# A two-layer attention kernel on one core: three accumulating transfers and five GpSimd additions a chunk, and a reordered passage between the layers

## The reference

```python
x = x + L0(_gn(x)); x = x + L1(_gn(x))
# _gn: subtract the mean and divide by the deviation over (H, W, 6 channels), for 32 groups
# L0, outlook attention: a = softmax over 9 taps of x @ W_attn (6 heads); v = x @ W_v
#   y[pos, head] = sum over the 9 taps of a[pos, head, tap] * v[pos + tap]; then y @ W_proj
# L1, shifted 7x7 window attention, 12 heads of 16: q, k, v; softmax(q k / 4 + bias + mask) v; then a projection
```

## Time and profile before

| what | value |
|---|---|
| median of three runs | 3894.26 us |
| profiled execution: its own time, its span | 3895.59 us, 3893.4 us |
| granted TensorE clock, mean | 0.941 of full |
| PE, DVE, ACT, POOL busy | 3493.4, 2794.1, 1905.6, 2423.8 us |
| one pass of the loop (first L1305 at 234.4, last at 3557.3 us, 7 passes between) | 474.7 us |
| in the second pass: outlook stage, passage to the first scores | 572.7 to 709.2 us, 709.2 to 743.8 us |

### The profile page before, as it was taken

How to read it: one execution, slowest core, us unless ns; L and a number is a source line. 1 busy time by engine, 2 the same in 40 slices (tenths; PEclk the granted TensorE clock), 3 DMA queues, 4 the chain that set the end, 5 groups by cost and what they waited for, 6 DMA issues and landing times.

```text
span 3893.4 us, 107608 instructions
## 1 busy us (share of the span) xinstructions
PE 3493.4 (90%) x39716; PEld 1962.9 (50%) x39716; DVE 2794.1 (72%) x4865; ACT 1905.6 (49%) x4034; POOL 2423.8 (62%) x1878
## 2 busy tenths in 40 slices
PE   3989989899798997989989899899998989988998
PEld 3346643466444664346633566335663356533665
DVE  2967759677596776957769577686767767687775
ACT  2435644355443654345643465435554355543565
POOL 0667737677375773757737577376764667555774
PEclk8999989899898998989989899899999999998998
DMA  3642217322272223712236122461225512164121
GB/s 77 132 87 64 78 45 139 74 66 80 59 139 62 71 68 74 141 49 77 75 71 135 48 72 76 88 127 49 75 62 100 113 52 78 55 121 93 60 73 58
DMA packets 206334, 317.58 MB, mean 82 GB/s; under 512 B 18904, under 2 KB 178136, under 8 KB 205784
## 3 DMA queue, kind: packets, MB, share of 16 engines
q0 software_dynamic: 31104, 148.65, 19.5%
q1 hardware_dynamic: 168992, 160.51, 13.9%
q10 hardware_dynamic: 5688, 1.11, 0.2%
HBM read 45.97 MB, written 38.54 MB: 22 GB/s over the span
## 4 chain that ended last, share of the span: by engine, by line
PE 59%; issue 11%; DVE 11%; ACT 8%; POOL 6%; DMA 2%; ACTq 0%; DVEq 0%; POOLq 0%
PE P L433 5%; PE P L625 5%; PE P L642 4%; PE P L294 4%; PE P L296 4%; PE P L596 4%; DVE prod L1280 3%; PE P L575 3%; PE P L303 3%; PE P L578 2%; PE P L302 2%; PE P L660 2%; POOL sp__70 L1566 2%; ACT kbd L988 2%; PE P L297 2%
## 5 line engine op out<-in xcount | busy, mean ns | idle before, releaser
L1559 POOL TENSOR_TENSOR sp__70<-sp__70,mx 128x588 f32<-128x588 f32 x512 | 600.7, 1173 | 622.0 <-DVE mx L1351 621.3
L1280 DVE TENSOR_TENSOR prod<-P,vpad 128x896 f32<-128x896 f32 (+1 forms) x784 | 802.0, 1046 | 133.0 <-PE P L433 120.6
L1566 POOL TENSOR_TENSOR sp__70<-sp__70,rc 128x588 f32<-128x588 f32 x512 | 601.6, 1175 | 55.3 <-DVE rc L1361 55.3
L1341 DVE TENSOR_TENSOR sp__70<-P,relb 128x196 f32<-128x196 f32 x512 | 184.5, 360 | 499.5 <-PE P L596 499.3
L1015 ACT ACTIVATE pt<-P 98x294 f32<-98x294 f32 x1024 | 431.3, 422 | 199.8 <-PE P L625 197.1
L1480 POOL DMA_DIRECT2D prod<-prod x216 | 202.7, 958 | 499.1 <-DVE prod L1280 495.7
L433 PE MATMUL P<-at,sel 108*128 108x448 bf16 x1512 | 426.4, 361 | 58.7 <-DVE prod L1280 30.5
L625 PE MATMUL P<-ident,sp__70 113*98 113x113 f32 x3072 | 399.2, 267 | 48.6 <-POOL sp__70 L1566 35.8
L1358 DVE TENSOR_REDUCE sm<-sp__70 128x12 f32<-128x588 f32 x512 | 387.2, 756 | 45.1 <-ACT sp__70 L1005 44.7
L625 PEld LDWEIGHTS P<-ident,sp__70 113*98 113x98 f32 x3072 | 329.7, 131 | 145.0 <-POOL sp__70 L1566 71.4
L1351 DVE TENSOR_REDUCE mx<-sp__70 128x12 f32<-128x588 f32 x512 | 389.5, 761 | 9.4
(11 more groups left out here) (197 smaller groups left out, 7503.1 us busy)
## 6 DMA issues: line engine op xcount, KB each, us to landing
prod<-prod POOLq DMA_DIRECT2D x216, 672.0 KB, 5.4
vbd<-vs SPq DMA_DIRECT2D x512, 147.0 KB
xin<-in_x SPq DMA_DIRECT2D x126, 336.0 KB, 4.1
out<-ot SPq DMA_DIRECT2D x184, 168.0 KB, 2.3
out<-ot SPq DMA_DIRECT2D x80, 84.0 KB
wn<-in_L_conv_qkv_weight SPq DMA_DIRECT2D x2, 432.0 KB, 6.4
wno<-in_L_conv_proj_weight SPq DMA_DIRECT2D x2, 144.0 KB, 6.5
self<-in_sel ACTq DMA_DIRECT2D x3, 91.1 KB
```

The lines of the kernel that those rows point to most:

```text
L1280: tt(by_row(dst), by_row(P[:, b:b + len(op), 0:CT]), val, ALU.mult).then_inc(prod_ok, 1)
L1559: tt(per_head(sp_[:, b, :]), per_head(sp_[:, b, :]), spread(mx[:, b, :]), ALU.subtract).then_inc(t_sub, 1)
L1566: tt(per_head(sp_[:, b, :]), per_head(sp_[:, b, :]), spread(rc[:, b, :]), ALU.mult).then_inc(p_norm, 1)
```

## The change

Two things are changed together. In the outlook stage the fourth transfer goes (MERGES = 3) and slots 6 and 7 are each added by POOL, so that there are five additions a chunk; for the last chunk the products of tap 8 stay in PSUM and DVE adds slots 7 and 6 and `psum_p` to them there, while POOL makes one addition in place of three. In the passage, a mean of the groups is estimated from the first four chunks during the last one (`mu0`), the final moments about it need one round of matmuls, each tile is aggregated as soon as its statistics are there, the normalization of row 0 is shared between DVE and ACT, keys are made before queries, the first exponentials come before the values are kept, and the second half of row 0's values moves into step 4 of row 0.

```diff
-MERGES = 4
+MERGES = 3
+TAIL, EARLY = 7, 4
-FREED = {0: 1, 2: 1, 3: 2, 4: 3, 6: 4}
+FREED = {0: 1, 2: 1, 6: 2, 3: 3, 4: 4, 7: 5}
...
+            def over_group(j, dst, src):
+                for n, (block, k) in enumerate(GROUPS[j]):
+                    last = mm(dst, gm[:, block, :], src(k), start=(n == 0), stop=(n == len(GROUPS[j]) - 1))
...
# PE, outlook(c), last chunk
+                        elif n in (4, 5, 6):
+                            estimate(n - 4)
+                            if n == 11:
+                                pe.wait_ge(e_kept, ONE + i + 1)
                             stay_warm(2, SOFT_BANK)
...
-                stay_warm(6, SOFT_BANK)
-                group_means(2 * i + 1, SOFT_BANK)
-                group_variances(2 * i + 1, SOFT_BANK)
+                stay_warm(10, SOFT_BANK)
+                group_moments()
                 stay_warm(8, 0)
...
# PE, window stage
@@ ring @@
-                        pe.wait_ge(vs_kept, ONE + 4 * (R + 1))
+                        pe.wait_ge(vs_kept, ONE + 4 * R + (4 if w else 2))
                     elif s == 4:
+                        pe.wait_ge(k_kept, ONE + T * (R + 1) + 3)
...
+                        else:
+                            window_values(0, 1, (R0, R1))
@@ start of the window stage @@
+                first_keys((0, 1))
+                keys_middle(0, 2)
                 queries_wide(0, (R0, R1))
                 queries_middle(0, TURN_BANK)
-                keys_wide(0, (0, 1))
-                keys_middle(0, 2)
                 pe.wait_ge(vs_zero, ONE + 3 * i + 3)
                 for s in range(AHEAD):
                     scores(0, s)
                 window_values(0, 0, (R0, R1))
-                window_values(0, 1, (TURN_BANK, Y_BANK))
-                pe.wait_ge(vs_kept, ONE + 4 * NW * i + 4)
# ACT
-                deviation(2 * i + 1, SOFT_BANK)
+                act.wait_ge(g_two, ONE + 3 * (i + 1))
+                go(gstd[:], gsq[:], ACT.Sqrt, bias=eps_s[:]).then_inc(g_std, 1)
...
+                go(xw[:, 0, 0, :]..., xa[:, 0, ...]..., ACT.Identity, bias=gb[:, 0:1], scale=ga[:, 0:1]).then_inc(xw_zero, 1)
                 load_table(4 * i + 3, ACT.Exp)
...
+                keep_keys(0, 0, 0)
+                keep_keys(0, 1, 1)
+                keep_keys(0, 2, 2)
                 keep_queries(0, 0, R0)
                 keep_queries(0, 1, R1)
                 keep_queries(0, 2, TURN_BANK)
...
+                exp_step(0, 0)
+                exp_step(0, 1)
                 act.wait_ge(vs_zero, ONE + 3 * i + 2)
                 for m in range(2):
                     keep_window_values(0, 0, m, (R0, R1)[m])
# DVE, product and finish_last of the last chunk
+                    if k == KK - 1 and c == LAST:
+                        tt(by_row(P[:, b:b + len(op), 0:CT]), by_row(P[:, b:b + len(op), 0:CT]), val, ALU.mult
+                           ).then_inc(prod_ok, 1)
+                        return
...
+                    two, one = P[:, 0:2, 0:CT], P[:, 2, 0:CT]
+                    tt(two, two, seven[:, 0:2, :], ALU.add).then_inc(tail_ok, 1)
+                    tt(one, one, seven[:, 2, :], ALU.add).then_inc(tail_ok, 1)
+                    tt(two, two, six[:, 0:2, :], ALU.add).then_inc(tail_ok, 1)
+                    tt(one, one, six[:, 2, :], ALU.add).then_inc(tail_ok, 1)
+                    dve.wait_ge(padd_ok, ONE + PADD * (G + 1))
+                    for j in (1, 0, 2):
+                        tt(y0[:, j, :], P[:, j, 0:CT], psum_p[:, j, :], ALU.add).then_inc(tail_ok, 1)
# DVE, in the last chunk after operation 2: three bn_aggr over EARLY chunks; after operation 8: mu0 <- PSUM
+                def moments():
+                    g = 2 * i + 1
+                    tt(gd[:, :, 0], mv[:, :, 0], mu0[:], ALU.subtract).then_inc(g_dev, 1)
+                    tt(gdev[:], gd[:, :, 0], gd[:, :, 0], ALU.mult).then_inc(g_dev, 1)
+                    tt(gd[:, :, 1], gdev[:], mv[:, :, 1], ALU.add).then_inc(g_sq, 1)
+                    mean, square = (P[:, SOFT_BANK, e:2 * T:2] for e in range(2))
+                    nc.vector.tensor_copy(gmean[:], mean).then_inc(g_two, 1)
+                    tt(gdev[:], gmean[:], gmean[:], ALU.mult).then_inc(g_two, 1)
+                    tt(gsq[:], square, gdev[:], ALU.subtract).then_inc(g_two, 1)
+                    tt(gmean[:], gmean[:], mu0[:], ALU.add).then_inc(g_dev, 1)
...
-                for j in range(T):
+                for j in (1, 2):
# POOL
+                    if k in (2, 4):
+                        pool.wait_ge(merged[k // 2], 16 * (G + 1))
+                    else:
                         pool.wait_ge(prod_ok, ONE + NOPS * G + LAST_OP[k] + 1)
...
                 def outlook(c):
                     if c > 0:
-                        add(c - 1, 1, 8)
-                        add(c - 1, 2, 4)
+                        add(c - 1, 2, 8)
+                        add(c - 1, 3, 4)
                     merge(c, 0)
+                    if c == LAST:
+                        merge(c, 1)
                     if c > 0:
-                        add(c - 1, 3, 6)
-                    merge(c, 1)
+                        add(c - 1, 4, 7)
+                    if c < LAST:
+                        merge(c, 1)
                     merge(c, 2)
                     add(c, 0, 2)
-                    if c < CHUNKS - 1:
-                        merge(c, 3)
+                    if c < LAST:
+                        add(c, 1, 6)
...
+                pool.wait_ge(merged[2], 16 * (G0 + CHUNKS))
+                tt(psum_p[:], psum_p[:], slot(4), ALU.add).then_inc(padd_ok, PADD - 1)
```

More of the change, by code:

```diff
@@ L117, in mixer @@
         gmean = sb("gmean", [128, T])
+        mu0 = sb("mu0", [128, T])
+        gd = sb("gd", [128, T, 2])
         gsq = sb("gsq", [128, T])
@@ L304, in middle @@
                 return mm(P[HI, bank, 0:n], w[:, 2, col:col + 64], src[:, 2], start=False, stop=True)
[L306 to L311, removed]
+            GROUPS = (((0, 0), (4, 1)), ((1, 1), (3, 0), (6, 2)), ((2, 2), (5, 1)))
+            def over_group(j, dst, src):
+                for n, (block, k) in enumerate(GROUPS[j]):
+                    last = mm(dst, gm[:, block, :], src(k), start=(n == 0), stop=(n == len(GROUPS[j]) - 1))
                 return last
@@ L315, in group_means @@
                 pe.wait_ge(g_agg, ONE + T * (g + 1))
-                over_groups(bank, 0, mv[:, :, 0]).then_inc(g_mean, 1)
+                for j in range(T):
+                    last = over_group(j, P[:, bank, j:j + 1], lambda k: mv[:, k, 0:1])
+                last.then_inc(g_mean, 1)
             def group_variances(g, bank):
                 pe.wait_ge(g_sq, ONE + g + 1)
-                over_groups(bank, T, gsq).then_inc(g_var, 1)
+                for j in range(T):
+                    last = over_group(j, P[:, bank, T + j:T + j + 1], lambda k: gsq[:, k:k + 1])
+                last.then_inc(g_var, 1)
             def stay_warm(n, bank):
@@ L511, in project, with estimate, group_moments @@
                         project_middle(1)
+                def estimate(j):
+                    if j == 0:
+                        pe.wait_ge(e_agg, ONE + T * (i + 1))
+                    last = over_group(j, P[:, SOFT_BANK, j:j + 1], lambda k: mv[:, k, 0:1])
+                    if j == T - 1:
+                        last.then_inc(g_mean, 1)
+                def group_moments():
+                    pe.wait_ge(g_sq, ONE + 2 * i + 2)
+                    for j in range(T):
+                        last = over_group(j, P[:, SOFT_BANK, 2 * j:2 * j + 2], lambda k: gd[:, k, :])
+                    last.then_inc(g_var, 1)
                 def outlook(c):
@@ L1042, in ring @@
                             keep_out(w - 2, 3, R1)
+                    elif s == 4:
+                        if w == 0:
+                            for m in range(2):
+                                keep_window_values(0, 1, m, (R0, R1)[m])
                     elif s == 5:
@@ L1103, in _ @@
                     keep_window_values(0, 0, m, (R0, R1)[m])
-                exp_step(0, 0)
-                for m in range(2):
-                    keep_window_values(0, 1, m, (TURN_BANK, Y_BANK)[m])
-                exp_step(0, 1)
                 for w in range(NW):
@@ L1288, in outlook @@
                             stat_x1(c - 2, n // 5)
+                        if c == LAST and n == 2:
+                            dve.wait_ge(x1_stat, ONE + T * (G0 + EARLY))
+                            nc.vector.memset(fence[:], 0.0)
+                            for j in range(T):
+                                nc.vector.bn_aggr(mv[:, j, :], stats[:, j, 0:EARLY, :].rearrange("p c s -> p (c s)")
+                                                  ).then_inc(e_agg, 1)
+                        elif c == LAST and n == 8:
+                            dve.wait_ge(g_mean, ONE + 2 * i + 2)
+                            nc.vector.tensor_copy(mu0[:], P[:, SOFT_BANK, 0:T]).then_inc(e_kept, 1)
                         if more:
```

(9 more changed lines are left out.)

88 lines of the change are left out of this document (43 added, 45 removed).

## The result

The changed kernel takes 3923.42 us, median of four runs (3921.29 to 3925.81), against 3893.32 us before in the same comparison: a ratio of 1.008, 95% interval 1.0065 to 1.0095. It is 30 us slower. The profiled execution, the fastest of the four, has a span of 3919.4 us, 26.0 us more than before.

What follows compares the result with a forecast made beforehand. POOL waiting on its own transfer was taken to bound the outlook stage: +13.8 us there, -11.0 in the passage, +2.8 a pass, times 8 = +22 on 3895, rounded to 3920 us; range 3850 to 3965.

Steps and rivals of the forecast that it cites:

- The bound: Outlook stage: POOL waits for its own transfer in a ring of 19.6 us, DVE's period; that idle time cannot be filled.
- The signs named ahead: Outlook stage: POOL's first addition every 21.9 us, released by DMA; DVE waits 2.3 us a chunk; last product at 150 us.
- The ring's size: Outlook stage: POOL part 15.9 us plus landing 5.83 to 6.1, taken as 21.9 us; last product +13.8 us a pass.
- What the ring consists of: Outlook stage: POOL's additions and transfer 1 with its landing; transfer 0 counted only as an issue of 0.61 us.
- The price list: Trainium skill's fit for a GpSimd transfer: 3.6 us, ring about 20.1 us, total 3848 us; traced shortest landing 5.2 us.
- (a to c): Passage from D, the last product's end: sums in PSUM -4.5 us, projection at full clock -1.0, single moments round -4.5.
- (d, e): Passage, into row 0: keys first -0.9 us, exponentials ahead of the copies of values -3.9 us.
- (f): Row 0: second half of values in step 4, so PE waits for their copies; +3.8 us, bounds +1 and +6.
- Total of the passage: From last product through row 0, gains less what row 0 gives back: -11.0 us a pass, -8 to -13.5.
- the ring is hidden or short: Rival, outlook stage: ring under 21.3 us, faster; 3848 us at 20.1 us, 3807 us wholly hidden; chance 0.23.
- stalls cool PE in the outlook stage: Rival: PE waits some 2.3 us in each chunk and its clock drops, much slower, 3970 us; chance 0.12.

Runs made afterwards that it cites:

- e5: Changed kernel with transfer 0 issued ahead of the addition of tap 4 and transfer 1 ahead of that of tap 7, same instructions; 3829.38 us.
- e6: Changed kernel with transfer 1 carrying one of its three tiles, the other two left out of the sum; 3832.75 us.
- e3: Kernel before with three transfers and five additions, keeping its own last chunk and passage; 4004.73 us, ratio 1.0286.
- e1: Changed kernel with transfer 1 issued right behind transfer 0, ahead of the last addition, in all chunks but the first; 3906.96 us.
- e10: e9 with queries ahead of keys and the first exponentials among the copies of values, as in the kernel before; 3823.49 us.
- e9: Changed kernel with four transfers and four additions again, and both halves of row 0's values made before the row; 3806.72 us.
- e2: Changed kernel with its fourth transfer and four additions back, keeping the new passage; 3812.63 us, ratio 0.9801.
- e4: Changed kernel with both halves of row 0's values made before the row, as in the kernel before; 3918.12 us.
- e8: Changed kernel with four transfers and four additions, and both transfers issued early as in e5; 3812.78 us, ratio 0.9799.

## Why the prediction was right

The forecast was 3920 us, slower, by +2.8 us a pass; it is 3923.4 us and +3.8 (30.1 / 8), or +3.3 in the profiled execution. The direction and the bound were reasoned out and the runs bear them out. That the total is met within 4 us is in part luck: the outlook stage lost 15.5 us a pass where 13.8 were forecast, the rest gained 12.2 (11.7 - 1.1 + 1.6) where 11.0 were, and the two errors, 14 and 10 us in the total, nearly cancel. Step by step:

- **The bound.** Right, and shown twice (`e5`, `e6`). POOL at 62% had no room in this order of work, because its idle time lay between the issue of its own transfer and the landing. "Cannot be filled" went too far: `e5` puts additions there, and the same five fit into DVE's 19.6 us. The signs named ahead are all in the trace: the recurrence of 21.8 us, the DMA as the releaser, the waits of DVE on slots 0 and 3 (here 1.6 + 1.6 and 1.4 + 1.6, forecast 2.3 together), the last product ending 151.8 us after the first began (forecast 150).
- **The ring's size.** The POOL part was forecast at 15.9 us and is 630.10 - 614.19 = 15.91. The landing was mis-sized: taken as 5.83 to 6.1 us, it was 6.80, 5.86, 5.89, 6.36 and 6.48 us in the five rings of the second pass, 6.28 in the mean. So the ring had 22.2 us and not 21.9, and the stage lost 15.5 us and not 13.8. The price in time, with the code of the passage unchanged, was 14.1 (`e3`).
- **What the ring consists of.** Here a step was incomplete: the prediction let it begin at transfer 1, and called transfer 0 an issue of 0.61 us. `e1` failed by that. In the changed kernel it made no difference in chunks 1 to 5, as transfer 0 goes out 3.6 us earlier, as it did before. In the last chunk the two go out together and the addition comes 8.4 us after the second. So POOL's last sum was done 3.6 us after the last product in the second pass and not 1.7, and DVE waited 0.52 us for it, where I had no wait.
- **The price list.** By the fit that the Trainium skill gives in "DMA: Bandwidth & Descriptors", in the anatomy of a DMA issued by GpSimd, such a transfer takes an estimated 3.6 us, and the change would have been a gain. The shortest landings are 5.2 us for 672 KB and, in `e6`, 3.1 us for 224 KB. An estimate from these two is a slope of 448 KB in 2.1 us and a fixed part of about 2.0 us. Two transfers in a row agree with the slope: in `e1` they land 3.3 us apart, for 672 KB each. The fixed part is that of the Trainium skill, the rate half of it. The measurement decides; that the halved rate is due to the accumulation is my guess and was not tested. (Two slips of the prediction change nothing: with the 3.6 us the ring would be 15.9 + 3.6 + 0.4 = 19.9 us and not 20.1, and 651.18 to 652.27 is 1.09 us and not 1.05.)
- **Sums, projection, moments (a to c).** Forecast `y0` complete at D + 5.2 and first matmul of row 0 about 10 us earlier than D + 25.2: measured D + 5.4 (732.35) and D + 15.0 (742.00), with D = 726.99. From `y0` to the round of moments it is 5.9 us in place of 6.5 (forecast -1.0, so 0.4 less won), from there to the first matmul 3.8 in place of 8.95 (forecast -4.5, so 0.7 more), at a granted clock of 1.00 in both stretches, where it was 0.84 and 0.63. No run takes a, b and c apart. PSUM costs DVE nothing more as a destination: 1.09 us, as in the products.
- **Keys and exponentials first (d, e).** First transposition forecast 32 us after D, measured 30.8 in the fifth pass: -15.9 against a forecast sum of -14.8. The stretches come out as forecast: 742.00 to 750.44 is 8.4 us (8.5), and from there to the first transposition, 758.73, it is 8.3 (8.1). But the second is won by something else than I said. `e10` has 37.1 (-9.6, from a to c, forecast -10), the two orders together gave 1.9 more where 4.8 were forecast (`e9`, 35.2), and the rest, 3.7 to 4.8 (`e2`, `e4`), comes from moving the values, which I had listed only as a cost. No run moves the values with the old place of the exponentials, so whether the one needs the other is open.
- **Given back in row 0 (f).** Forecast +3.8, bounds 1 and 6; measured 15.9 at the first transposition less 10.4 at step 7, +5.5 in the fifth pass and +5.1 in the mean of passes 2 to 8. The wait for the copies, forecast 3.4 us, shows as 2.29 us in the second pass, 1.10 in the fifth and at most 0.44 in the others. The failed step is the other half: I called the values in step 4 hidden, since POOL sets the pace in steps 0 to 5, and did not ask who waits for them. POOL itself does, 4.04 us in every pass.
- **Total of the passage.** Forecast -11.0, measured -10.0 a pass alone (`e2`), with the 1.3 us that the new last chunk costs there.

The rivals: that the ring is hidden or short (0.23) is refuted by the trace, and what such a ring gives is in `e5`, 3829 us and not the 3807 put on it; that stalls cool PE in the outlook stage did not happen, its clock is 1.00 in the stretch above.

## What to carry to other kernels

An engine that issues transfers and then waits for them can be the bound at 62 to 64% busy: follow its own chain from one issue through the landing back to the same issue, and compare that ring with the period of the stage, before giving it more to do. When the ring is too long, move the issues forward ahead of work that does not need them, all transfers that share the queue and not only the one waited for; the same work in another order was worth 94 us here. Stop when the ring is under the period: a shorter one gave nothing more (`e8`). And work moved off the start of a stage is won only if nobody waits for it later: ask for its readers and for whoever wants to overwrite what it reads.

## What the runs showed unforeseen

The end of a pass is 1.6 us shorter in the changed kernel, with none of its code changed. TensorE's granted clock in the same steps, in two stretches of 10 us that begin 4.6 us after the last addition of scores of the fifth pass (columns as in the earlier trace rows), before:

```profile
2430.00:2440.00 10.00, 7.54 (x83) 6.39 (x81) 1.85 (x7) 7.08 (x13) 2.00 (x3) 0.55 0.19 56
2440.00:2450.00 10.00, 8.53 (x67) 3.29 (x67) 0.46 (x1) 2.65 (x7) 0.00 (x0) 0.60 0.03 10
```

and after:

```profile
2451.00:2461.00 10.00, 6.23 (x83) 5.28 (x82) 1.83 (x6) 7.83 (x16) 2.00 (x3) 0.77 0.20 56
2461.00:2471.00 10.00, 9.35 (x73) 3.63 (x73) 0.46 (x1) 2.40 (x5) 0.00 (x0) 0.72 0.04 10
```

0.55 and 0.60 of full against 0.77 and 0.72, so the lower level of 1.2 GHz covers less of them. The fifth pass is the widest case: over the 20 us it has 0.57 against 0.74, and most passes of the changed kernel have 0.66. In the kernel before, the seventh pass has the short end (43.4 us) as well, and the versions of this study change between 43.1 and 45.9 us from pass to pass. In `e4` and `e5` the ends of 45.1 to 45.6 us follow window stages some 1.5 us shorter, so part of it only moves between the two. The clock is the likely cause and not a shown one: the third pass of the kernel before has 0.66 too, and yet a long end of 45.4 us. Why the clock drops later in some passes was not tried; nothing in the change aims at it.

Two transfers issued 0.6 us apart cost the second one's user 8.3 us, issued 3.6 us apart 5.9 us (`e1`, and above), so a transfer issued early behind another gains only part of its lead.
